# Two attention layers and two feed-forward layers on one core: tokens in two halves, attention units between the feed-forward steps

## The chip, the core and the metric

The kernel runs on one core of a Trainium2 chip. Its engines work side by side, each through its own list of instructions in order, and meet at semaphores: TensorE (PE, matrix products into the eight PSUM banks), VectorE (DVE), ScalarE (ACT), GpSimd (POOL, no PSUM) and SyncE (SP, here only DMA issues). The metric is the device time of one execution in microseconds.

## What is computed

Four residual steps on 1,024 tokens (16 sequences of 64) of width 256:

```python
x = x + tanh(g_xattn[0]) * L0_xattn(layernorm(x), ctx, ctx)
x = x + tanh(g_ffn[0])   * L0_ffn(layernorm(x))
x = x + tanh(g_xattn[1]) * L1_xattn(layernorm(x), ctx, ctx)
x = x + tanh(g_ffn[1])   * L1_ffn(layernorm(x))
...
# L0_xattn: 32 query heads of width 8 share 8 key heads; keys and values are ctx (64 keys)
# L0_ffn, hidden width 704, W = (wq - 128) * scale:
out = qlinear(silu(gate) * up, wq_down, s_down)
# L1_xattn: 16 query heads of width 16 share 4 key heads, then
out @ Wc.T + bc
# L1_ffn, 32 experts of inner width 96, every expert on every token:
sel_w, sel_e = top_k(x @ gate_w.T, 8); sel_w = softmax(sel_w)
h = silu(g) * u * masked_w[:, :, None]
out = einsum('tei,ehi->th', h, w_down_proj)
```

## The kernel before

It is written engine by engine, and the order on each engine is the order of the code. Four stages follow one another: attention of layer 0, its feed-forward, attention of layer 1, its experts.

*Attention.* Tokens lie in eight tiles of 128 (two sequences each). A tile has four units of work in layer 0 and two in layer 1. A unit is a chain: scores on PE (`scores`, L1055, two of 512 columns), row maximum and shift on DVE (L734, L739), exponential on ACT (L576), four transposes on PE (L1064), their copy on ACT (L582), four value products on PE (`values`, L1080). Per sequence DVE divides by the row sums (`normalise`, L754 and L762). Scores and transposes each use two banks in turn, and scores run two units ahead of the transposes. Per tile come the next layer's statistics (`next_stats`, `next_mean`, L780 to L784), a power on POOL for 1/std (L405), the normalised tile `xm` (L789), its transposes (L1105), and its split into a high and a low part, `xh` and `xl` (L435, L438 on POOL). POOL also makes the block-diagonal keys (`keys`, L337) and splits the queries (L412, L415). The statistics of the first normalisation (`ln_stats`, L709 to L714) are taken for six tiles at once ahead of the loop. `over_tiles` sets how the units of neighbouring tiles interleave; layer 1 adds a projection (L1096) and the routing logits (L1027).

*Feed-forward.* Full precision is made from three products (`product`, L1002 to L1004): high x high, high x low, low x high. The hidden width goes in chunks of 128 (6 in layer 0, 24 in layer 1), the tokens in two blocks of 512. One chunk on one block is a step: 6 products each for gate, up and down, down one step behind. ACT takes silu of the gate (L632) and rounds h to its high part `hh` (L655); DVE multiplies with up (L959, or L883 and then L888 with the expert mask) and makes the low part `hl` (L893). Weights stream in once, chunk by chunk; ACT rounds the high part `wh` (L551) and POOL subtracts the low part `wl` (L427), and both blocks use them. The accumulators of both blocks hold four banks; transposes bring the result back, and DVE adds it to x (L976).

*Routing.* Between attention and experts DVE picks the eight largest logits (L908 to L923); PE spreads the weights to 16 masks (L1177), which ACT and DVE copy to SBUF (L646, L935). They stay there, in `mbc`.

Of the kernel before, what the change touches and what calls it, by code (L numbers as in the profile page):

```python
# [23 lines left out]
NBLK = TOK // BLK  # L34
# [5 lines left out]
MOE_CHUNKS = EXPERTS * INNER // P  # L40
WPACK = 3 * DM
WRING = 3
# [3 lines left out]
FFN_CHUNKS = (HIDDEN + P - 1) // P  # L46
NEG = -3.0e38
W_EARLY = (TT - 2, TT - 1)
MASK_BANKS = (4, 7, 5, 6)
MASKS = NBLK * EXPERTS // EPQ  # L50
KEYS_AFTER = {3: (0, 2), 4: (2, 4), 5: (4, TT)}
AHEAD = 2


def after(eng, sem, value):

    if not (isinstance(value, int) and value <= 0):
# [61 lines left out]
class Attention:  # L119

    def __init__(self, layer, kv_heads, kbd, vbd, sb, sem):  # L130
# [1172 lines left out]
```

## Time and profile before

| | |
|---|---|
| runs | 450.45, 447.51, 449.8 us (median 449.8) |
| span of the profiled execution | 450.2 us; its own time is not listed apart, and the span lies within the runs |
| busy | PE 399.1, DVE 296.7, ACT 198.7, POOL 180.4 us |
| mean granted PE clock | 0.965 |

Records of PE overlap, since a product starts before the one ahead of it has drained, so its busy time is more than its work. On the other engines busy time is the sum of their instructions.

### The profile page before, as it was taken

How to read it: one execution, taken by the hardware profiler on the slowest of the kernel's cores; microseconds unless marked ns; L12 is line 12 of the kernel's file. 1: busy time of each engine (PE TensorE's matmuls, PEld its weight loads, DVE VectorE, ACT ScalarE, POOL GpSimd, SP SyncE). 2: the span in 40 equal slices, each digit the busy share in tenths (PEclk: the TensorE clock that was granted, in tenths of full speed). 3: DMA queues.
4: the chain of work that ended last, by engine and by line, in shares of the span. 5: the costliest groups of instructions: out<-in, count | busy, mean ns of one | idle time of the engine just before them, and what ended most of it. 6: DMA issues, size and time to landing. Idle time of an engine off the chain costs nothing.

```text
span 450.2 us, 6432 instructions
## 1 busy us (share of the span) xinstructions
PE 399.1 (89%) x2032; PEld 327.9 (73%) x2032; DVE 296.7 (66%) x554; ACT 198.7 (44%) x382; POOL 180.4 (40%) x174
## 2 busy tenths in 40 slices
PE   0598888959999778898877999999999999999994
PEld 0497777848888478787664887887887887887883
DVE  5989899843555778996465366566566566566554
ACT  6465455735444635554136333433433433333332
POOL 8776667561788353447500231131131121221200
PEclk9999899998999989999688899999999999999999
DMA  6500000110202000001100112112112011111002
GB/s 169 133 1 2 1 0 1 35 37 1 71 0 95 0 0 2 1 1 35 37 0 0 36 35 71 35 35 73 35 36 69 35 40 65 35 43 62 0 1 93
DMA packets 10711, 15.99 MB, mean 36 GB/s; under 512 B 4097, under 2 KB 6657, under 8 KB 10689
## 3 DMA queue, kind: packets, MB, share of 16 engines
q1 hardware_dynamic: 10688, 15.71, 11.8%
q8 instruction: 12, 0.20, 0.2%
q14 instruction: 11, 0.08, 0.1%
HBM read 14.66 MB, written 1.05 MB: 35 GB/s over the span
## 4 chain that ended last, share of the span: by engine, by line
PE 72%; DVE 15%; issue 5%; POOL 4%; ACT 2%; DVEq 1%; DMA 1%; POOLq 0%; ACTq 0%
PE bank L1002 19%; PE bank L1003 18%; PE bank L1004 18%; PE bank L1080 5%; PE bank L1055 4%; PE bank L1064 3%; DVE mx L734 2%; DVE dt_pt L739 2%; DVE xn L722 1%; POOL rstd L405 1%; DVE yt L762 1%; PE bank L1027 1%; DVE x L976 1%; PE bank L1040 1%; PE bank L1096 1%
## 5 line engine op out<-in xcount | busy, mean ns | idle before, releaser
L427 POOL TENSOR_TENSOR wl<-wraw,wh 128x768 fp32r<-128x768 f32 x24 | 44.7, 1863 | 162.2 <-ACT wh L551 162.2
L1002 PE MATMUL bank<-xh,wh 128*128 128x512 f32 x240 | 96.3, 401 | 0.0
L1003 PE MATMUL bank<-xl,wh 128*128 128x512 f32 x240 | 95.6, 398 | 0.0
L1004 PE MATMUL bank<-xh,wl 128*128 128x512 f32 x240 | 95.5, 398 | 0.0
L655 ACT ACTIVATE hh<-h_t 128x512 fp32r<-128x512 f32 x60 | 37.9, 632 | 114.9 <-DVE h_t L888 101.3
L893 DVE TENSOR_TENSOR hl<-h_t,hh 128x512 fp32r<-128x512 f32 x60 | 48.6, 810 | 42.7 <-ACT hh L655 42.7
L883 DVE TENSOR_TENSOR t_t<-bank,pts 128x512 f32<-128x512 f32 x48 | 33.2, 692 | 43.5 <-PE bank L1004 42.1
L888 DVE TENSOR_TENSOR h_t<-t_t,vbd 128x512 f32<-128x512 f32 x48 | 53.4, 1113 | 3.1 <-DVE t_t L883 1.0
L1055 PE MATMUL bank<-kbd,qt 128*128 128x256 f32 (+2 forms) x128 | 36.8, 395 | 20.2 <-DVE dt_pt L739 17.3
L1002 PEld LDWEIGHTS bank<-xh,wh 128*128 128x128 f32 x240 | 46.5, 194 | 9.9 <-issue 0.2
L1004 PEld LDWEIGHTS bank<-xh,wl 128*128 128x128 f32 x240 | 46.3, 193 | 10.1
L1003 PEld LDWEIGHTS bank<-xl,wh 128*128 128x128 f32 x240 | 46.3, 193 | 9.5
L1002 PE MATMUL bank<-hh,wh 128*128 128x512 f32 x120 | 50.4, 420 | 2.6 <-DVE hl L893 1.6
L1080 PE MATMUL bank<-vbd,pts 128*128 128x128 f32 (+1 forms) x384 | 52.3, 281 | 0.0
L1080 PEld LDWEIGHTS bank<-vbd,pts 128*128 128x128 f32 x384 | 49.3, 197 | 2.0 <-issue 0.3
L1003 PE MATMUL bank<-hl,wh 128*128 128x512 f32 x120 | 47.8, 398 | 0.0
L1004 PE MATMUL bank<-hh,wl 128*128 128x512 f32 x120 | 47.5, 396 | 0.0
L582 ACT ACTIVATE pts<-bank 128x256 f32<-128x256 f32 x96 | 31.6, 381 | 35.3 <-PE bank L1064 35.3
L1055 PEld LDWEIGHTS bank<-kbd,qt 128*128 128x128 f32 x128 | 19.9, 204 | 25.2 <-DVE dt_pt L739 7.6
L632 ACT ACTIVATE pts<-bank 128x512 f32<-128x512 f32 x48 | 28.3, 592 | 20.4 <-PE bank L1004 20.4
L734 DVE TENSOR_REDUCE mx<-bank 128x8 f32<-128x512 f32 x48 | 32.9, 685 | 2.0 <-PE bank L1055 1.2
L739 DVE TENSOR_TENSOR dt_pt<-bank,mx 128x512 f32<-128x512 f32 x48 | 33.1, 689 | 1.5
(104 smaller groups left out, 577.9 us busy)
## 6 DMA issues: line engine op xcount, KB each, us to landing
wraw<-w SPq DMA_DIRECT2D x30, 384.0 KB, 3.1
out<-x SPq DMA_DIRECT2D x8, 128.0 KB, 1.8
x<-x_in SPq DMA_DIRECT2D x1, 768.0 KB, 6.8
ctx_k<-ctx_t SPq DMA_DIRECT2D x2, 256.0 KB, 3.8
ctx_v<-ctx_in SPq DMA_DIRECT2D x2, 256.0 KB, 8.3
x<-x_in SPq DMA_DIRECT2D x1, 256.0 KB, 2.7
wc<-wc_t SPq DMA_DIRECT2D x1, 256.0 KB, 2.9
vbd<-sel_in SPq DMA_DIRECT2D x1, 256.0 KB, 3.5
```

What stands on the lines that cost most here:

```text
L427: nc.gpsimd.tensor_tensor(wl[:, cc % WRING, :], src[:, cc % 2, :], wh[:, cc % WRING, :].bitcast(F32), ALU.subtract).then_inc(m.w_split, 1)
L655: nc.scalar.activation(hh[:, k, :], h_t[:, k, :], ACT.Copy).then_inc(m.hh_ready, 1)
L734: chain.mark(nc.vector.reduce_max(mx[:, k, :], s, AX.X))
L739: nc.vector.tensor_tensor(dt_[:, k, :].rearrange("p (h t) -> p h t", t=KEYS), s, mx[:, k, :].unsqueeze(2).to_broadcast([P, 8, KEYS]), ALU. ...
L883: nc.vector.tensor_tensor(t_t[:], bank[2 + k][:], s_t[:, k, :], ALU.mult).then_inc(m.t_done, 1)
L888: nc.vector.tensor_tensor(h_t[:, k, :], t_t[:], mbc[:, q, k * BLK:(k + 1) * BLK], ALU.mult).then_inc(m.h_full, 1)
L893: nc.vector.tensor_tensor(hl[:, k, :], h_t[:, k, :], hh[:, k, :].bitcast(F32), ALU.subtract).then_inc(m.h_split, 1)
L1002: nc.tensor.matmul(o, wh[:, s, w_sl], rh, start=first, stop=False, skip_group_check=reopened)
L1003: nc.tensor.matmul(o, wh[:, s, w_sl], rl, start=False, stop=False, skip_group_check=reopened)
L1004: return nc.tensor.matmul(o, wl[:, s, w_sl], rh, start=False, stop=last, skip_group_check=reopened)
L1055: last = nc.tensor.matmul(bank[u % 2][:, i * a.ns:(i + 1) * a.ns], qt[:, b2, 2 * gp:2 * gp + 2, :].rearrange("p g s -> p (g s)"), a.kbd[:, ...
L1080: last = nc.tensor.matmul(bank[4 + b2][:, gp * P:(gp + 1) * P], pts[:, k, j, :], a.vbd[:, 2 * t + b2, pair, :], start=(pair == 0), stop=(p ...
```

## The change

The tokens go in two halves of 512. A feed-forward layer takes all its chunks for the first half and then again for the second: four passes, 60 steps (`PASS`: 0 to 5 and 6 to 11 for layer 0, 12 to 35 and 36 to 59 for layer 1). Attention is cut in ticks, one per unit and a few more to drain. Tables of numbers say which ticks stand after a step's gate products and which after its down products. Layer 0's ticks 0 to 21 run alone, 22 to 37 within steps 0 to 5; layer 1's ticks of the first half run within steps 9 to 11, the last six behind step 11 (`TAIL`), those of the second half within steps 16 to 32. DVE, ACT and POOL run one tick ahead of PE.

Layer 0's quantised weights are kept in six slots; layer 1's are loaded twice, and rounded and split twice. One bank each holds gate (`GB`), up (`UB`) and the mask, and two hold a pass's sum (`DB`), so that attention keeps banks of its own (`SB`, `PB`, `VB`, `MB`); up to unit 19 it borrows more to alternate. Silu is written with tanh, which takes one more instruction on DVE (`gate`). The mask of an expert group is spread into its bank when needed, and DVE reads it there (`weigh`). The low part of x moves to DVE (`x_low`); the first statistics are taken tile by tile; value blocks shrink from 128 to 72 columns; keys go in a ring of three tiles; all loops are written out.

```diff
-WRING = 3
-MASK_BANKS = (4, 7, 5, 6)
-AHEAD = 2
+HT = TT // 2
+VW = 72
+RING = 3
+SLOTS = 6
+WRAW = 3
+PASS = ((0, F0), (F0, 2 * F0), (2 * F0, 2 * F0 + MC), (2 * F0 + MC, 2 * F0 + 2 * MC))
+GB, UB, MASK = 0, 1, 7
+DB = ((2, 3), (2, 3), (2, 3), (4, 5))
+SB, PB, VB, MB = 4, 5, 6, 7
+TWO = 20
+ALONE = 22
...
+TAIL = ((11, 12), (13, 14, 15, 16))
+ROUTE = (13, 34)
...
+            def w_low(i):
+                src = wf[:, i % 2, :] if i < F0 else wraw[:, i % WRAW, :]
+                pool.wait_ge(F.wh_ready, i + 1)
+                slot = (i if i < F0 else i - F0) % SLOTS
+                ops.tensor_tensor(wl[:, slot, :], src, wh[:, slot, :].bitcast(F32), ALU.subtract
+                                  ).then_inc(F.w_split, 1)
...
-                    nc.scalar.activation(s_t[:, k, :], bank[k][:], ACT.Silu, scale=scale).then_inc(m.s_ready, 1)
+                nc.scalar.activation(s_t[:, s % 2, :], bank[GB][:], ACT.Tanh,
+                                     scale=sgh[:, c:c + 1] if s < MOE0 else 0.5).then_inc(F.s_ready, 1)
...
+            def x_low(a, t):
+                dve.wait_ge(a.xh_ready, t + 1)
+                tok = slice(t * P, (t + 1) * P)
+                ops.tensor_tensor(xl[:, :, tok], bank[a.x_bank(t)][:, 0:DM].rearrange("p (k c) -> p k c", c=P),
+                                  xh[:, :, tok].bitcast(F32), ALU.subtract).then_inc(a.xl_ready, 1)
...
+            def gate(s):
+                k = s % 2
+                dve.wait_ge(F.s_ready, s + 1)
+                ops.scalar_tensor_tensor(t_t[:, k, :], s_t[:, k, :], 1.0, bank[GB][:], ALU.add, ALU.mult
+                                         ).then_inc(F.sg_done, 1)
...
-                    nc.vector.tensor_tensor(h_t[:, k, :], t_t[:], mbc[:, q, k * BLK:(k + 1) * BLK], ALU.mult
-                                            ).then_inc(m.h_full, 1)
+                ops.tensor_tensor(h_t[:, k, :], bank[MASK][:], t_t[:, k, :], ALU.mult).then_inc(F.h_full, 1)
...
+            def tick0(n):
+                a, (t, u) = A[0], divmod(n, 4)
+                if u == 2 and t + 1 < TT:
+                    q_transposes(a, t + 1)
+                if u == 1 and 0 <= t - 2 < TT:
+                    x_transposes(a, t - 2)
+                if n + 1 < a.total:
+                    scores(a, n + 1)
+                if 0 <= n - 2 < a.total:
+                    values(a, n - 2)
+                if n < a.total:
+                    p_transposes(a, n)
...
+            q_transposes(A[0], 0)
+            scores(A[0], 0)
+            for n in range(ALONE):
+                tick0(n)
+            for s in range(STEPS):
+                gate(s)
+                if s in START:
+                    scores(A[1], START[s] * 2 * HT)
+                for k, n in beside(s, 0):
+                    tick(k, n)
+                up(s)
...
+                if s and s != MOE0:
+                    down(s - 1)
...
+                for k, n in beside(s, 1):
+                    tick(k, n)
...
+            down(STEPS - 1)
+            back(3)
```

PE at the passage from layer 0's attention to its feed-forward. In the rows 1055 and 1019 are scores, 1064 and 1037 transposes of a unit, 1080 and 1054 values, 1105 and 1090 transposes of x. Before:

```order
L1105 MATMUL bank<-ident,xm 128x128 x2
L1080 MATMUL bank<-vbd,pts 128x128 x4
L1064 MATMUL bank<-ident,dt_pt 128x128 x4
L1080 MATMUL bank<-vbd,pts 128x128 x8
L1105 MATMUL bank<-ident,xm 128x128 x2
L1002 MATMUL bank<-xh,wh 128x512
L1003 MATMUL bank<-xl,wh 128x512
```

And now, within step 1:

```order
L1153 MATMUL bank<-xh,wl 128x512
L1090 MATMUL bank<-ident,xm 128x128 x2
L1019 MATMUL bank<-kbd,qt 128x512 x2
L1054 MATMUL bank<-vbd,pts 128x72 x4
L1037 MATMUL bank<-ident,pt 128x128 x4
L1151 MATMUL bank<-xh,wh 128x512
L1152 MATMUL bank<-xl,wh 128x512
L1153 MATMUL bank<-xh,wl 128x512
L1151 MATMUL bank<-xh,wh 128x512
L1152 MATMUL bank<-xl,wh 128x512
L1153 MATMUL bank<-xh,wl 128x512
L1151 MATMUL bank<-hh,wh 128x512
```

Before, the products (1002 to 1004) began when the last units had drained; now transposes, scores and values of a unit (1090, 1019, 1054, 1037) stand between gate and up.

DVE in the expert stage; 883 and 862 multiply with up, 888 and 868 with the mask, 893 and 873 are the low part of h. Before:

```order
L893 TENSOR_TENSOR hl<-h_t,hh 128x512
L883 TENSOR_TENSOR t_t<-bank,pts 128x512
L888 TENSOR_TENSOR h_t<-t_t,vbd 128x512
L893 TENSOR_TENSOR hl<-h_t,hh 128x512
L883 TENSOR_TENSOR t_t<-bank,pts 128x512
```

And now, in step 17, with a unit of layer 1:

```order
L873 TENSOR_TENSOR hl<-h_t,hh 128x512
L850 SCALAR_TENSOR_TENSOR t_t<-s_t,bank 128x512
L862 TENSOR_TENSOR t_t<-bank,t_t 128x512
L868 TENSOR_TENSOR h_t<-bank,t_t 128x512
L730 TENSOR_REDUCE mx<-bank 128x8
L746 RECIPROCAL rc<-bank 128x8
L751 TENSOR_TENSOR yt<-bank,rc 64x2x4x16 x2
L736 TENSOR_TENSOR dt_<-bank,mx 128x512
```

A step has gained line 850, and behind the weighting stand the maximum, the division and the shift of a unit.

DVE at the end of layer 0's feed-forward; 985 and 880 scale the output, 976 and 887 add it to x, 709 to 714 and 711 to 716 are statistics. Before:

```order
L893 TENSOR_TENSOR hl<-h_t,hh 128x512
L976 TENSOR_TENSOR x<-bank,x 128x256 x2
L709 BN_STATS stats<-x 128x6 x2
L712 BN_AGGR mv<-stats 128x2 x2
L714 TENSOR_SCALAR ve<-mv 128x2
L985 TENSOR_SCALAR dt_pt<-bank,sdt 128x512
L722 TENSOR_SCALAR xn<-x,mv,rstd 128x4x4x16
L976 TENSOR_TENSOR x<-bank,x 128x256 x6
L722 TENSOR_SCALAR xn<-x,mv,rstd 128x4x4x16
L709 BN_STATS stats<-x 128x6 x6
L712 BN_AGGR mv<-stats 128x2 x6
L714 TENSOR_SCALAR ve<-mv 128x6
```

And now, behind step 11:

```order
L873 TENSOR_TENSOR hl<-h_t,hh 128x512
L880 TENSOR_SCALAR ot<-bank,sdt 128x512
L775 TENSOR_SCALAR xm<-x,mv,rstd 128x256
L781 TENSOR_TENSOR xl<-bank,xh 128x2x128
L761 SCALAR_TENSOR_TENSOR x<-bank,tg,xb 128x256
L767 BN_STATS stats<-x 128x6
L768 BN_AGGR mv<-stats 128x2
L769 TENSOR_SCALAR ve<-mv 128x1
L887 TENSOR_TENSOR x<-bank,x 128x256 x4
L711 BN_STATS stats<-x 128x6 x2
L714 BN_AGGR mv<-stats 128x2 x2
L716 TENSOR_SCALAR ve<-mv 128x2
```

Before, the second attention began here; now its first half ends here, and its last residual and statistics (761, 767) stand ahead of the additions and of the second half's statistics.

## Rows read from the trace of the kernel before

**Rows 1.** The page's totals: busy us, share of the span, instructions.
```profile
PE 399.1 (89%) x2032; PEld 327.9 (73%) x2032; DVE 296.7 (66%) x554; ACT 198.7 (44%) x382; POOL 180.4 (40%) x174
```

**Rows 2.** PE in order of time: start, us, engine, line, operation, tiles, shapes.
```profile
299.23 0.39 PE L1002 MATMUL bank<-xh,wh 128*128 128x512 f32 x1
...
300.59 0.39 PE L1002 MATMUL bank<-hh,wh 128*128 128x512 f32 x1
```

**Rows 3.** The chain of waits in layer 0's attention: start, us, engine, tile, line.
```profile
78.69 0.46 PE bank L1055 x2
...
79.59 0.89 PE bank L1080 x8
80.48 0.45 PE bank L1064 x4
```

**Rows 4.** The same chain at the routing logits.
```profile
201.62 2.14 PE bank L1027 x18
```

**Rows 5.** Busy time by stage: window, length, then each engine; PE's clock share, DMA.
```profile
18.50:101.50 83.00, 71.04 (x493) 62.67 (x493) 68.84 (x150) 46.63 (x114) 53.39 (x56) 0.98 0.04 11
101.50:151.10 49.60, 48.20 (x206) 39.50 (x206) 25.04 (x28) 24.73 (x37) 31.80 (x27) 0.97 0.12 38
151.10:220.00 68.90, 57.26 (x409) 51.42 (x409) 56.67 (x152) 33.70 (x80) 33.74 (x47) 0.96 0.04 12
220.00:247.30 27.30, 22.53 (x75) 15.65 (x75) 14.23 (x48) 11.69 (x22) 3.73 (x5) 0.75 0.00 0
247.30:439.00 191.70, 191.70 (x818) 153.32 (x819) 113.65 (x136) 69.40 (x113) 41.04 (x22) 0.99 0.13 41
```

**Rows 6.** Line 893 alone (DVE's low part of h) in one window.
```profile
252.00:435.00 183.00, 29.78 (x43) 1.00 0.14 43
```

**Rows 7.** Groups by line and shape: count, busy us, mean ns, idle before.
```profile
L427 POOL TENSOR_TENSOR wl<-wraw,wh 128x768 fp32r<-128x768 f32 x24 | 44.7, 1863 | 162.2 <-ACT wh L551 162.2
...
L959 DVE SCALAR_TENSOR_TENSOR h_t<-bank,su,pts 128x512 f32<-128x512 f32 x12 | 9.0, 750 | 14.9 <-PE bank L1004 14.9
```

**Rows 8.** DVE in order of time, layer 0's attention.
```profile
39.83 0.40 DVE L789 TENSOR_SCALAR xm<-x,mv,rstd 128x256 f32<-128x256 f32 x1
...
43.08 0.69 DVE L739 TENSOR_TENSOR dt_pt<-bank,mx 128x512 f32<-128x512 f32 x1
...
48.55 1.98 DVE L789 TENSOR_SCALAR xm<-x,mv,rstd 128x256 f32 x1 [0.55 <-POOL rstd L405]
...
53.37 0.69 DVE L739 TENSOR_TENSOR dt_pt<-bank,mx 128x512 f32<-128x512 f32 x1
...
66.08 0.26 DVE L754 RECIPROCAL rc<-bank 128x16 f32<-128x16 f32 x1
66.26 0.37 DVE L780 BATCH_NORM_STATS2 stats<-x 128x6 f32 x1
66.66 0.59 DVE L762 TENSOR_TENSOR yt<-bank,rc 64x128 f32<-64x128 f32 x2
67.28 0.69 DVE L739 TENSOR_TENSOR dt_pt<-bank,mx 128x512 f32<-128x512 f32 x1
67.89 0.17 DVE L783 BATCH_NORM_AGGREGATE mv<-stats 128x2 f32<-128x6 f32 x1
68.10 0.15 DVE L784 TENSOR_SCALAR ve<-mv 128x1 f32<-128x1 f32 x1
```

**Rows 9.** POOL in order of time, beside the second xm of rows 8.
```profile
48.48 1.90 POOL L337 TENSOR_TENSOR kbd<-kh,a_kmask 128x1024 f32 x1
```

**Rows 10.** ACT in order of time, the first exponential.
```profile
18.40 0.63 ACT L576 ACTIVATE dt_pt<-dt_pt 128x512 f32<-128x512 f32 x1 [0.56 <-DVE dt_pt L739]
```

**Rows 11.** SP's queue at the end.
```profile
444.66 3.79 SPq L393 DMA_DIRECT2D out<-x  x8
```

**Rows 12.** Busy time and clock around the first expert products.
```profile
217.40:227.60 10.20, 10.20 (x34) 8.32 (x34) 2.84 (x7) 0.77 (x2) 5.30 (x8) 0.50 0.00 1
```

**Rows 13.** Line 893 over the whole span: shortest, median and longest in ns.
```profile
L893 DVE TENSOR_TENSOR hl<-h_t,hh x60: 680/693/1914, 106.4 to 441.1; 128x512 fp32r<-128x512 f32 x60
```

More of the change, by code:

```diff
@@ L33 @@
 BLK = 512
-NBLK = TOK // BLK
 EXPERTS = 32
@@ new lines, in _ @@
+            act.wait_ge(k_loaded, 32)
+            copy(kh[:, 0:4], ctx_k[:, 0:4]).then_inc(kh_ready, 1)
+            copy(kh[:, 4:BATCH], ctx_k[:, 4:BATCH]).then_inc(kh_ready, 1)
+            q_copy(A[0], 0)
+            act.wait_ge(g_loaded, 32)
+            nc.scalar.activation(tg[:], tg[:], ACT.Tanh).then_inc(tanh_ready, 1)
+            act.wait_ge(tanh_ready, 1)
+            act.wait_ge(v_loaded, 32)
+            values(A[0])
+            for n in range(ALONE + 1):
+                tick0(n)
@@ new lines, in scores @@
+            def scores(a, n):
+                t = a.tile(n)
+                if n % a.units == 0:
+                    if a.layer == 0:
+                        pe.wait_ge(a.k_ready if t else k0_ready, 2 * t if t else 2)
+                    else:
+                        pe.wait_ge(a.k_ready, 2 * (t + 1))
+                    pe.wait_ge(a.q_ready, t + 1)
+                if a.before(n) >= 0:
+                    pe.wait_ge(a.sub_done, a.before(n) + 1)
+                if a.layer == 1 and n == 2 * HT:
+                    pe.wait_ge(a.xl_ready, HT)
+                b2, gps = a.part(n)
+                slot = (a.layer * TT + t) % RING
+                for i, gp in enumerate(gps):
+                    for r in range(2):
+                        done = nc.tensor.matmul(bank[a.s_bank(n)][:, i * a.ns:(i + 1) * a.ns],
+                                                qt[:, t % 2, b2, 2 * gp:2 * gp + 2, :].rearrange("p g s -> p (g s)"),
+                                                kbd[:, slot, r, b2, 0:a.ns], start=(r == 0), stop=(r == 1))
+                done.then_inc(a.scored, 1)
@@ new lines, in values @@
+            def values(a, n):
+                b2, gps = a.part(n)
+                t = a.tile(n)
+                q = 2 * t + b2
+                if n == 0:
+                    pe.wait_ge(a.v_ready, a.hk)
+                    pe.wait_ge(a.ones_ready, a.hk)
+                if gps[0] == 0 and a.v_before(q) >= 0:
+                    pe.wait_ge(a.y_done, a.v_before(q) + 1)
+                for j in range(4):
+                    gp, pair = gps[j // a.npair], j % a.npair
+                    if j in (0, 2):
+                        pe.wait_ge(a.pts_ready, 2 * n + 1 + j // 2)
+                    done = nc.tensor.matmul(bank[a.v_bank(q)][:, gp * P:gp * P + VW], pts[:, n % 2, j, :],
+                                            a.vbd[:, q, pair, :], start=(pair == 0), stop=(pair == a.npair - 1))
+                done.then_inc(a.av_done, 1)
```

1660 lines of the change are left out of this document (829 added, 831 removed).

## The prediction

> **What bounds the kernel now.** I first read the page's totals. PE counts as busy for 399.1 of 450.2 us [rows 1], but two records overlap, so I went by spacing: in the steady expert stage six products stand 1.36 us apart, 0.227 us each [rows 2]. A step (one hidden chunk, one block of 512 tokens) is 18 of them, 4.09 us. Twelve steps of layer 0 and 48 of layer 1 are 1,080 products, 245 us. A unit of attention takes 0.46 for scores, 0.89 for values and 0.45 for transposes [rows 3]; with the transposes of queries and of x, at 0.11 us per 128 columns by the last of these rows, it takes about 1.97, so 32 units are 63 us. Layer 1 has 16 units of about 1.9, plus per tile a projection of about 0.9 (an estimate: four records, each of twice the columns of a values record), logits of 6 x 0.119 [rows 4] and 0.9 of transposes: 50 us. Masks and the transposes back add 8. Together PE has 366 us of work, and 84 us in which it waits or runs slowly.
>
> The Trainium skill (Trainium Kernel Development and Optimization, Performance Expectations) calls matmul busy time a bad metric, because matmuls are pipelined. The trace agrees: by the busy row at most 51 us could be won, by spacing 84.
>
> The stages show where those 84 us lie [rows 5]. Layer 0's attention (18.5 to 101.5) holds 66 us of PE work (3 of them early products) in 83; there DVE is busy 68.84 and is the bound. Layer 0's feed-forward is 49.6 for about 45. From 151.1 to 220 the second attention holds some 50 in 68.9, with DVE busy for 56.67. Routing and masks (220 to 247.3) hold 13 in 27.3, at a mean clock of 0.75. The expert stage wastes little: 43 steps in 183 us, 4.26 each against 4.09 [rows 6]. The rest is the start (18.5) and the tail (11.2).
>
> **The change, part by part.** The work on PE stays the same. Values are written 72 columns wide instead of 128, which I count at nothing: logits with only 32 moving columns still take 0.119 us a record [rows 4], no less than the 0.111 of a values record (0.89 for 8). Reading the weights twice adds no visible wait while a step lasts 4 us: POOL's low part, 1.86 us [rows 7], is then due once per step instead of once per two, and the products of the step ahead hide it. Without that cover the 24 more of them would cost 24 x 1.86 = 45 us.
>
> *DVE* gets one instruction more per step, (tanh+1) x gate, at 0.75 like the nearest form [rows 7]: 60 x 0.75 = 45 us. In layer 0 it is all added. In layer 1, three full-width instructions and the low part are 0.75 + 3 x 0.7 = 2.85, less than a step. The mask now comes from PSUM and no longer from SBUF. Tanh and exp need no table switch: the new ScalarE order holds a single table load.
>
> *Attention alone (units 0 to 21).* One tile of before, from shift to shift, lasts 53.37 - 43.08 = 10.3 us [rows 8]. Inside it xm took 1.98 instead of the 0.4 it takes elsewhere, right behind POOL's key product [rows 8, 9]. After, each tile has its own statistics on DVE, three small instructions spaced 0.40 + 0.21 + 0.10 [rows 8] (before did six tiles at the start), and x's low part, a 128x256 read of PSUM, half a shift, so 0.4. A tile gets 10.3 + 0.75 + 0.4 + 0.2 for a scores product that is now one unit ahead instead of two = 11.6. At the start the first exponential (18.40, [rows 10]) moves little, since the work ahead of it stays; the shorter lead costs the first tile about 2, and I put tile 1 at 26.3. Tile 1 has no x of two tiles ago: 10.2. Tiles 2 and 4: 11.6 each. Tile 3: 11.6, plus 1.9 for the scale and selector preparation that moves here, plus 1.0 for a low-part product queued on POOL ahead of the addition that DVE waits for. Units 20 and 21 and the part of 22 that the first gate product waits for: 8.6. The first gate starts at 26.3 + 56.5 = 82.8.
>
> *Steps 0 to 5 with units 22 to 37.* In one step PE runs gate, unit n, up, down, units n+1 and n+2. Scores now have one bank, so scores of n+3 wait for the shift of n+2: that is maximum 0.6, normalise 0.8 to 0.9 and shift 0.6 on DVE behind the scores of n+2 [rows 8], and it ends some 1.3 us after PE has run out of other work. PE work of 4.09 + 3 x 1.97 = 10.0 becomes 11.1. Three such steps, then 7.4 for step 3 (units that only drain), 2 x 4.2, and 1.2 for the last low part of x: 50.3, to 133.1.
>
> *Steps 6 to 8.* 4.1; 4.1 + 2.1 for the transposes back of the first half, which alternate with DVE additions; 4.6. Sum 14.9, to 148.0.
>
> *Steps 9 to 11 with layer 1's first half.* Eleven units; the full ones cost DVE 1.25 for maximum and shift, 0.85 normalise, and up to 1.2 of residual, statistics and apply. One after another on single banks they take 8.4, 15.4 and 15.5 us where PE has 33: 39.3, to 187.3.
>
> *Drain and routing.* Six more units, the transposes back and the second half's statistics form one chain on DVE: low part, output scaling, last residual and its statistics, four additions, four statistics, apply, low part, logits. I count 13.8 us. Steps 12 and 13 cannot go down before the routing weights: 12.1 for 8.2 of products. To 213.2. Before paid from 149 to 163 and from 220 to 247 for the same things.
>
> *Steps 14 to 35 with the second half.* One unit per step. PE has 4.09 plus 1.0 to 2.8. DVE's loop for a heavy unit is 3.45 for the unit, then exp and tanh on ScalarE (0.63 each [rows 10], 1.45 with hand-over), then 0.75 + 0.7 + 0.7: 7.05. Only one unit is that heavy; the others are light on DVE or drain only, so PE sets them. By unit: 48.5 for eight steps, 47 for nine, 9.2 for the two ahead, 1.6 for masks, 14.4 for the last three with routing in them: 120.7, to 333.9.
>
> *Steps 36 to 59.* 24 x 4.09 + 8 masks x 0.23 + 1.6 for one way back = 101.7, to 435.6. Each gate waits for DVE's previous one, which ends some 1.1 us before it is needed, so the single banks cost nothing here.
>
> *The tail.* SP spends 3.79 us on eight stores [rows 11], now four are left at the end: 11.2 - 1.9 = 9.3 behind the last up product, which ends 1.2 before the step does: 443.7.
>
> *Clock.* Before ran at half clock (1.2 GHz) throughout 217.4 to 227.6 [rows 12], after 4 us of sparse transposes. The drain at 187 to 213 is just as sparse. I add 3 us, with bounds of 0 (no lower clock where PE is critical) and 7 (10 us like these, at half rate, less what DVE hides). Sum 446.7 against its own span of 450.2, to which next to nothing lies around it; the median of the runs shown is 449.8, 0.4 below it. I forecast **446 us**.
>
> So the profit is only 4 us: the way from attention to feed-forward and routing gets shorter, and layer 0's attention pays some of it back, because the woven units still go at DVE's pace.
>
> **Rivals.** (a) *Weaving hides fully.* If DVE keeps ahead of PE in every woven step, steps 0 to 5 take 45.6, 9 to 11 33 and 14 to 35 116: 15 us less, 431. For it: DVE is busy for only about two thirds of the span. Against: DVE is nearly gapless in today's attention, and the scores bank is single.
>
> (b) *Weaving hides nothing.* Slower: in steps 0 to 2, 10, 11 and 18 to 23 the unit's DVE round simply adds to the 4.09 us, as it stands alone today: 10 units at 2.6 (10.3 / 4) and 16 at 3.3 instead of what I charged, 16 us more, 462. It decides where scores of unit n+1 wait for the shift of n before PE has a product left to run. Against it: gate, up and down stand between most units.
>
> (c) *POOL's low part blocks DVE's.* hl took 0.69 as a rule and 1.91 at worst [rows 13]. With a POOL product in every step, a late one would hold hl until it ends; h_split then comes 0.3 us too late beyond its slack of 0.9. At 48 steps that is 14 us, 461. By my order POOL's ends 0.2 us before hl is due, so it must run over 1.1 us late first. The Trainium skill (SBUF — State Buffer, SBUF: two separate sides) states this as an exclusive lock for a whole instruction between GpSimd and a DVE instruction with two SBUF inputs; by that rule the mask in PSUM frees the weighting, but hl stays exposed, now twice as often. The trace agrees that the two meet: xm took 1.98 behind a POOL product of 1.90 [rows 8, 9].
>
> (d) *It doesn't do what it says*, for instance a tick order that puts waits on banks that make halves serial. I see none in the order; 0.03.
>
> **How the numbers follow.** Forecast as summed, with its own range of 440 to 453 from the clock's bounds and 4 us either way for hand-worked steps: 0.45. (a) 0.22, (b) 0.22, (c) 0.08, (d) 0.03. About 1%, or 4.5 us, can be told from no change. Of the forecast's range four tenths lie below 445.3, so faster is 0.18 + 0.22 = 0.40; the other six tenths are same, 0.27; (b), (c), (d) are slower, 0.33. The range of 8 in 10 reaches to (a) and close to (b): 430 to 464.
>
> **What the profile after would show.** Right: the first product of a gate near 83 us, step 14 near 213, step 36 near 334, steps of 4.1 us from there, DVE gapless in the units alone, PE waiting for the shift in steps 0 to 2. Wrong: tiles alone under 10.5 or over 12.5; woven steps at PE's sum (a) or at PE plus DVE (b); hl well over 0.8 us in the last 24 steps (c); half clock longer than 10 us between 187 and 213.

## The result and the profile after

The changed kernel takes 475.57 us (median of 4 runs, 474.91 to 478.26) against 448.65 (median of 4, 447.51 to 450.45): the ratio is 1.059, with a 95% interval of 1.055 to 1.064. The forecast was 446, with a range of 430 to 464. The profiled execution has a span of 473.7 us and took 475.5.

The page's totals, which answer to [rows 1]:

```profile
PE 406.9 (86%) x2032; PEld 332.1 (70%) x2032; DVE 324.6 (69%) x638; ACT 205.5 (43%) x388; POOL 203.7 (43%) x181
```

All engines are busier in sum, and none has become a bound for the whole. Busy time by stage, as in [rows 5], cut where the first gate product of steps 0, 6, 9, 14 and 36 starts, at 187.20, where PE has done the products within step 11 and goes on with ticks 8 to 10, and at 464.50, behind the products of step 59. Columns: window, length, PE, PEld, DVE, ACT, POOL, granted clock, DMA share, GB/s.

```profile
0.00:82.26 82.26, 54.25 (x326) 47.23 (x327) 63.48 (x137) 47.51 (x104) 65.53 (x72) 0.92 0.29 79
82.26:136.50 54.24, 48.52 (x272) 41.27 (x272) 35.34 (x76) 22.77 (x48) 10.57 (x14) 0.94 0.01 1
136.50:151.39 14.89, 13.99 (x67) 11.35 (x67) 10.52 (x22) 4.49 (x7) 2.34 (x3) 1.00 0.00 0
151.39:187.20 35.81, 30.27 (x190) 26.49 (x188) 25.43 (x55) 18.79 (x40) 19.05 (x21) 0.95 0.05 13
187.20:230.96 43.76, 28.04 (x115) 21.41 (x113) 23.02 (x70) 7.71 (x16) 9.36 (x10) 0.71 0.09 27
230.96:359.83 128.87, 124.24 (x608) 99.97 (x607) 94.68 (x174) 57.42 (x103) 57.16 (x42) 0.98 0.22 68
359.83:464.50 104.67, 104.37 (x449) 82.54 (x447) 68.82 (x102) 45.51 (x70) 39.71 (x22) 1.00 0.26 77
464.50:473.70 9.20, 3.26 (x15) 1.87 (x14) 3.31 (x7) 1.32 (x2) 0.00 (x0) 0.90 0.17 58
```

Set against the forecast's own sums:

| stretch | forecast | measured |
|---|---|---|
| to the first gate product | 82.8 | 82.3 |
| steps 0 to 5 | 50.3 | 54.2 |
| steps 6 to 8 | 14.9 | 14.9 |
| steps 9 to 13, drain and routing of the first half | 65.2 | 79.6 |
| steps 14 to 35 | 120.7 | 128.9 |
| steps 36 to 59 | 101.7 | 104.7 |
| tail | 8.1 | 9.2 |
| clock, apart | 3 | in the rows above |
| span | 446.7 | 473.7 |

Half of the miss lies in steps 9 to 13. The forecast has three terms for them: steps 9 to 11 with ticks 0 to 10 (8.4 + 15.4 + 15.5 = 39.3), the drain (13.8), steps 12 and 13 (12.1). Cut at the start of step 11, at the end of tick 10 (the projection at 194.25 in the chain below) and at the first product of step 12, with the columns as above:

```profile
151.39:175.11 23.72, 19.95 (x138) 17.60 (x135) 17.04 (x37) 13.15 (x27) 13.95 (x16) 1.00 0.06 18
175.11:196.16 21.05, 16.95 (x89) 14.04 (x87) 12.05 (x31) 6.39 (x15) 6.35 (x7) 0.82 0.07 19
196.16:215.71 19.55, 10.29 (x44) 8.05 (x45) 9.36 (x29) 2.18 (x5) 3.25 (x3) 0.67 0.08 21
215.71:230.96 15.25, 11.13 (x37) 8.22 (x37) 9.99 (x29) 4.79 (x8) 4.85 (x5) 0.72 0.10 26
```

Steps 9 and 10 took 23.7 us, as forecast (8.4 + 15.4). Step 11 took 21.1 instead of 15.5, the drain 19.6 instead of 13.8, steps 12 and 13 15.3 instead of 12.1, and in these three the granted clock was 0.82, 0.67 and 0.72. What PE waited for from 187.2 to 230.96 (us in total, times, longest):

```profile
PE bank L1108 <- DVE xl L781: 7.4, 4, 3.5
PE bank L1151 <- DVE hl L873: 4.7, 2, 2.6
PE bank L1239 <- DVE wts L917: 1.5, 1, 1.5
PE bank L1220 <- DVE x L887: 1.4, 1, 1.4
```

The logits (1108) wait for the low part of x, tile by tile, and the products for the low part of h. The chain of waits there, start, us, what:

```profile
192.79 1.46 PE bank L1108 x6
194.25 1.91 PE bank L1077 x4
196.25 0.49 DVE x L761
196.77 0.44 DVE stats L767
197.52 0.69 DVE hl L873
...
203.32 0.84 PE bank L1108 x6
...
208.23 0.76 DVE stats L711 x2
209.54 0.66 DVE stats L711 x2
210.69 0.41 DVE xm L775
...
214.41 1.46 PE bank L1108 x6
```

The work passes from PE to DVE and back in pieces of half a microsecond to two. The six logits of a tile take 1.46 at 192.79 and 214.41 and 0.84 at 203.32: half clock (1.2 GHz) and full. Before, the same chains of projection, logits and routing are [rows 4] and [rows 12]; there eight tiles passed through them in a row. How long the drain is, PE's last transposes of a unit show, before and in the first half of the kernel after:

```profile
210.69 0.60 PE L1064 MATMUL bank<-ident,dt_pt 128*128 128x128 f32 x4
...
227.83 0.26 PE L1027 MATMUL bank<-gwh,xl 128*128 128x32 f32 x1
```

```profile
182.25 1.12 PE L1037 MATMUL bank<-ident,pt 128*128 128x128 f32 x4 [1.14 <-ACT pt L553]
```

From there to the end of the last logits (228.1 before, 215.9 after) it is 17.4 us before, with 12 products of the expert stage in it, and 33.6 us after, with 18 products of steps 10 and 11 in it.

What shows against the single steps of the forecast: the added instruction, line 850, takes 687 ns (first row), and the low part of h is as long as in [rows 13] in most steps, but has a longer worst case (second row; shortest, median and longest in ns).

```profile
L850 DVE SCALAR_TENSOR_TENSOR t_t<-s_t,bank x60: 673/687/691, 87.1 to 462.6; 128x512 f32<-128x512 f32 x60
L873 DVE TENSOR_TENSOR hl<-h_t,hh x60: 674/693/2352, 93.4 to 465.6; 128x512 fp32r<-128x512 f32 x60
```

And PE around a mask (1239) in step 36, in order of time:

```profile
362.33 0.39 PE L1153 MATMUL bank<-xh,wl 128*128 128x512 f32 x1
362.65 0.50 PE L1239 MATMUL bank<-wts,sel 64*128 64x512 f32 x1
363.07 0.51 PE L1151 MATMUL bank<-hh,wh 128*128 128x512 f32 x1
363.42 0.40 PE L1152 MATMUL bank<-hl,wh 128*128 128x512 f32 x1
363.65 0.40 PE L1153 MATMUL bank<-hh,wl 128*128 128x512 f32 x1
```

The starts are 0.23 apart between equal products, but 0.32, 0.42 and 0.35 around the mask: it costs 0.32 + 0.42 + 0.35 - 2 x 0.23 = 0.63, not one product of 0.23.

### The profile page after: what moved, and what is told of

It reads as the page before. It is cut to its first block, busy times and chain, and to the rows that moved or that the text cites. A ratio compares the mean times of both kernels' runs of the same rounds, so it can differ in the third digit from the quotient of the medians.

```text
span 473.7 us, 6122 instructions
## 1 busy us (share of the span) xinstructions
PE 406.9 (86%) x2032; PEld 332.1 (70%) x2032; DVE 324.6 (69%) x638; ACT 205.5 (43%) x388; POOL 203.7 (43%) x181
## 4 chain that ended last, share of the span: by engine, by line
PE 72%; DVE 16%; POOL 5%; issue 3%; ACT 2%; DMA 1%; DVEq 0%; POOLq 0%
PE bank L1151 18%; PE bank L1152 17%; PE bank L1153 17%; PE bank L1054 6%; PE bank L1019 4%; PE bank L1037 3%; DVE dt_ L736 3%; POOL kbd L338 2%; PE bank L1077 2%; DVE xm L775 2%; PE bank L1108 2%; PE bank L999 2%; PE bank L1239 1%; DVE hl L873 1%; DVE yt L751 1%
## 5 line engine op out<-in xcount | busy, mean ns | idle before, releaser
L436 POOL TENSOR_TENSOR wl<-wraw,wh 128x768 fp32r<-128x768 f32 x48 | 89.2, 1860 | 85.0 <-ACT wh L532 85.0
L1151 PE MATMUL bank<-xh,wh 128*128 128x512 f32 x240 | 100.2, 417 | 3.7 <-POOL wl L436 1.8
L850 DVE SCALAR_TENSOR_TENSOR t_t<-s_t,bank 128x512 f32<-128x512 f32 x60 | 41.1, 686 | 33.0 <-ACT s_t L632 32.4
L1054 PEld LDWEIGHTS bank<-vbd,pts 128*128 128x128 f32 x384 | 52.6, 203 | 4.9 <-DVE yt L751 1.8
L730 DVE TENSOR_REDUCE mx<-bank 128x8 f32<-128x512 f32 x48 | 33.1, 689 | 33.1 <-PE bank L1019 32.6
L1054 PE MATMUL bank<-vbd,pts 128*128 128x72 f32 x384 | 51.9, 281 | 1.3 <-DVE yt L751 1.3
L632 ACT ACTIVATE s_t<-bank 128x512 f32<-128x512 f32 x48 | 28.6, 596 | 45.8 <-PE bank L1153 45.8
L1019 PE MATMUL bank<-kbd,qt 128*128 128x512 f32 (+1 forms) x128 | 36.5, 390 | 12.9 <-DVE dt_ L736 11.1
L1037 PE MATMUL bank<-ident,pt 128*128 128x128 f32 x192 | 33.6, 303 | 16.2 <-ACT pt L553 14.7
L409 POOL TENSOR_TENSOR rstd<-ve,neghalf 128x1 f32<-128x1 f32 x16 | 10.9, 680 | 76.8 <-DVE ve L769 76.8
L553 ACT ACTIVATE pt<-dt_ 128x512 f32<-128x512 f32 x48 | 30.3, 632 | 27.7 <-DVE dt_ L736 27.4
## 6 DMA issues: line engine op xcount, KB each, us to landing
out<-x SPq DMA_DIRECT2D x8, 128.0 KB, 2.6
```

Of the source, the lines that this page charges most:

```text
L436: ops.tensor_tensor(wl[:, slot, :], src, wh[:, slot, :].bitcast(F32), ALU.subtract).then_inc(F.w_split, 1)
L553: nc.scalar.activation(pt[:, n % 2, :], dt_[:, n % 2, :], ACT.Exp, scale=a.scale).then_inc(a.p_ready, 1)
L730: return chains[a.layer].mark(ops.reduce_max(mx[:, n % 2, :], s, AX.X))
L850: ops.scalar_tensor_tensor(t_t[:, k, :], s_t[:, k, :], 1.0, bank[GB][:], ALU.add, ALU.mult).then_inc(F.sg_done, 1)
L1019: done = nc.tensor.matmul(bank[a.s_bank(n)][:, i * a.ns:(i + 1) * a.ns], qt[:, t % 2, b2, 2 * gp:2 * gp + 2, :].rearrange("p g s -> p (g s)"),
L1037: done = nc.tensor.transpose(bank[a.p_bank(n)][:, j * P:(j + 1) * P], pt[:, n % 2, j * P:(j + 1) * P], ident[:])
```

## The experiments

Theory A: layer 1's first half loses the time. Its chain from the last units to the first masks has too little beside it, and PE has more to do elsewhere than I had counted. Theory B: DVE's added work made the kernel slow. Theory C: weaving costs as much as it hides. The medians of the kernel before, taken with each group of runs, lie between 448.65 and 452.02 us, so the ratios to it are compared, and the lengths of stages in the traces. These vary too where an edit touches nothing: the first gate product falls between 81.5 and 85.5 us, steps 0 to 5 take 51.0 to 55.8, steps 9 to 13 78.2 to 81.0, steps 14 to 35 128.7 to 129.5. A difference inside such a range tells nothing; the forecast's 50.3 for steps 0 to 5 lies just outside of its range.

**The added instruction.** It is cut to one column, and the product with up takes tanh alone.

```diff
-ops.scalar_tensor_tensor(t_t[:, k, :], s_t[:, k, :], 1.0, bank[GB][:], ALU.add, ALU.mult
+ops.scalar_tensor_tensor(t_t[:, k, 0:1], s_t[:, k, 0:1], 1.0, bank[GB][:, 0:1], ALU.add, ALU.mult
```

> The kernel after with the extra DVE instruction of a step cut from 512 columns to one; the product with up then takes tanh alone, so (tanh+1) x gate is left out of the computation. It takes 59 x 0.6 = 35 us off DVE and hurts nothing else. Theory A (PE starves in the chain from the first half's last units to its masks, 187 to 231, and elsewhere has more work than I counted; DVE's load is not the bound): 466 to 472, since the instruction lies on a path only in the woven steps 0 to 5 and 9 to 11 and at two steps of the drain. Theory B (DVE's load, raised by this instruction, is what made the kernel slow): 455 or less.

475.06 us, ratio 1.052 (1.047 to 1.057). Steps 0 to 5 took 52.3 instead of 54.2, steps 9 to 13 79.5, steps 14 to 35 128.0. Theory B is out: 35 us taken from DVE give back 1.9, 0.1 and 0.9 us, and only the last is more than such stretches vary by. The 466 to 472 that stood with theory A was missed as well: even in the woven steps the instruction costs less than expected.

**Layer 0's units alone.**

```diff
-TWO = 20
-X_TWO = 4
-ALONE = 22
-BESIDE0 = {0: ((22,), (23, 24)), ...
+TWO = 32
+X_TWO = 8
+ALONE = 38
+BESIDE0 = {}
```

> The kernel after with all 38 ticks of layer 0 alone and two banks each to the end of layer 0's units, none beside steps 0 to 5. Woven, these six steps took 54.2 us after the first gate product at 82.3. Theory A: ten more units at 2.6 us (10.3 / 4), 3 us of drain and 6 x 4.1: step 6 begins near 136, the kernel takes 473 to 478, so weaving in layer 0 hides about nothing. Rival (weaving hides what DVE leaves open): step 6 begins at 145 or later, 484 or more. Third (the single banks of the woven units cost more than they hide): step 6 before 131, 470 or less.

476.22 us, ratio 1.055 (1.051 to 1.058). The first products of steps 0 and 6, in order of time (the file's lines are one less):

```profile
110.20 0.78 PE L1150 MATMUL bank<-xh,wh 128*128 128x512 f32 x1
...
135.71 0.39 PE L1150 MATMUL bank<-xh,wh 128*128 128x512 f32 x1
```

Step 6 starts at 135.7 instead of 136.5 (134.7 to 141.1 in woven runs with no edit in layer 0). In layer 0 the weave gains nothing that can be told. The run gives the units two banks each as well, so it doesn't separate what the weave hides from what its single banks cost.

**The second half's units alone.**

```diff
-BESIDE2 = {s: ((), (s - 16,)) for s in range(16, 33)}
+BESIDE2 = {16: ((), tuple(range(17)))}
```

> The kernel after with the 17 ticks of layer 1's second half all behind step 16, none beside steps 17 to 32. Woven, steps 14 to 35 took 128.9 us, of which 22 x 4.09 = 90 are products, and PE had hardly a wait. Theory A (here the weave hides DVE's rounds under the products): alone a tick goes at DVE's pace and 17 of them take 50 to 56 us instead of the some 29 that they add woven: 495 to 502. Rival (the weave hides nothing here either): 473 to 480.

497.41 us, ratio 1.099 (1.095 to 1.103). The first products of steps 16 and 17:

```profile
244.71 0.39 PE L1151 MATMUL bank<-xh,wh 128*128 128x512 f32 x1
...
301.07 0.77 PE L1151 MATMUL bank<-xh,wh 128*128 128x512 f32 x1
```

The 17 ticks take 56.4 - 4.1 = 52.3 us alone. Steps 14 to 35 took 151.2 instead of 128.9: here the weave does what it is for, and saves 22 us. Theory C holds for layer 0 only. The run tells more: eight units of one half, alone, take 52.3 us, while before 16 units took 68.9 [rows 5]. The two don't compare at the same clock: from 273.5 to 301.1, behind the last unit's transposes, PE ran at half clock in run e4, and was busy for 18.1 of these 27.6 us. At full clock it would be up to 9 us less (an estimate, half of the 18.1), 43 for half the units; so up to 9 of the 22 us are what the weave saves by keeping the clock up.

**The order in the drain.** First the second half's statistics go behind the routing (`route(0)`), then behind step 12's low part, then the ticks are spread, then both.

```diff
                     add_back(1)
-                    ln_stats(A[1], HT, HT + 2)
-                    ln_stats(A[1], HT + 2, TT)
                     for n in TAIL[1]:
...
-BESIDE1 = {9: ((), (0, 1)), 10: ((2, 3), (4, 5)), 11: ((6, 7), (8, 9, 10))}
-TAIL = ((11, 12), (13, 14, 15, 16))
+BESIDE1 = {9: ((0,), (1, 2, 3)), 10: ((4, 5, 6), (7, 8)), 11: ((9, 10), (11, 12))}
+TAIL = ((13, 14), (15, 16))
```

> The kernel after with the second half's statistics on DVE moved behind the first half's routing; they stood ahead of the normalisation of the first half's last tile (208.2 to 210.7). Theory A (the chain to the first masks is the bound there): 2.4 us less, 473. Rival (DVE waits for something else there, or the second half needs its statistics early): no change or slower, 475 to 478.

> The kernel after with the second half's statistics on DVE moved behind the low part of step 12 in step 13, where no step waits for them; behind the routing (run e3) they stood still ahead of step 12's instructions on DVE. Theory A: steps 11 to 14 take 53.4 us instead of 55.85, the kernel 473. Rival (that DVE time is not on the path, e3 moved nothing because something else ends there): 55.5 or more, 475 to 477.

> The kernel after with the ticks of layer 1's first half placed earlier among steps 9 to 11, so that products of steps 10 and 11 stand between the light ticks 11 to 14 that ran without cover. In after PE waited 5.5 us from step 9 to 187.2 and 15.7 from there to step 14. Theory A (the drain has no products to cover it): step 12 begins 5 to 10 us sooner after step 9 than the 64.3 us of after, the kernel takes 466 to 471. Rival (the rounds over DVE, ACT and POOL set the pace of every tick, wherever the products stand): what the drain saves the ticks ahead of it lose, step 9 to 12 stays at 62 to 66 us, 474 to 478.

> Runs e5 and e7 together. Theory A: both gains add, 463 to 469. Rival: 473 to 477.

None of the first three reached what theory A forecast. Behind the routing: 475.27 us, ratio 1.052 (1.050 to 1.055); steps 11 to 13 took 56.2 instead of 55.9, since the statistics still stood ahead of step 12 on DVE. Behind step 12: 474.41, ratio 1.051 (1.043 to 1.059); steps 11 to 13 54.3 (53.4 forecast), steps 9 to 13 77.9, hardly outside what they vary by. Spread: 472.40, ratio 1.050 (1.043 to 1.058); steps 9 to 13 75.8; step 12 begins 59.7 us behind step 9, 4.6 sooner, where theory A had 5 to 10 and the rival at most 2. Both: 468.67, ratio 1.038 (1.031 to 1.046); steps 9 to 13 (cut at step 12):

```profile
151.31:210.33 59.02, 46.88 (x268) 39.08 (x265) 37.34 (x86) 21.71 (x47) 23.88 (x26) 0.87 0.07 21
210.33:225.90 15.57, 11.85 (x36) 8.94 (x37) 10.87 (x38) 4.79 (x8) 2.54 (x2) 0.72 0.09 26
```

Together 74.6 instead of 79.6. That meets the forecast (463 to 469). Order gives back 5 of the 14.4 us that were missed.

**The clock in the drain.** Products that nobody reads are put where PE waited; then the same with run e8's order.

```diff
+def filler(k, o):
+    if o == GB:
+        pe.wait_ge(F.sg_done, MOE0)
+    for _ in range(k):
+        nc.tensor.matmul(bank[o][:], wh[:, 5, 0:P], xh[:, 0, BLK:2 * BLK], start=True, stop=True, ...)
...
+filler((4, 5, 12, 5)[t], GB)      # in logits of tiles 0 to 3
+filler(7, GB)                     # ahead of the last down product
+filler(4, GB)                     # ahead of back(1)
+filler(12, DB[2][0]), filler(6, ...), filler(8, ...)   # in step 13, around the routing
```

> The kernel after with 63 products more on PE, written to a bank that nobody reads before it is begun anew, at those places from 191 to 228 where PE waited (4 to 12 in each). They keep PE busy where it ran at half clock (1.2 GHz) from 198 to 219 and from 228 to 233. If the half clock costs what its records say (logits 1.46 instead of 0.84 per tile, projection 1.9 instead of 1.0, products 0.43 instead of 0.23): step 12 to 14 and the drain get 6 to 10 us shorter, 466 to 470. Rival (the lower clock falls only where PE waits for DVE anyway, or the products get in the way): 474 to 480.

> Run e8 with the filling products of run e6 (the four ahead of the first logits left out, 59 products). If the clock and the order are separate costs of the drain, both gains add: 461 to 465. If the better order has taken the same waits that the filling products fill, 466 to 470.

With filling alone 468.12 us, ratio 1.036 (1.028 to 1.043), and with both 467.09, ratio 1.037 (1.029 to 1.045). Steps 9 to 11 and 12 to 13, the filling alone:

```profile
151.94:211.60 59.66, 50.80 (x305) 42.66 (x303) 38.42 (x96) 21.52 (x47) 23.54 (x26) 0.97 0.07 21
211.60:227.02 15.42, 14.53 (x64) 10.86 (x64) 10.22 (x29) 4.79 (x8) 3.64 (x4) 1.00 0.08 27
```

And with run e8's order:

```profile
150.58:210.06 59.48, 51.97 (x300) 43.44 (x299) 37.17 (x86) 21.71 (x47) 23.88 (x26) 0.94 0.07 21
210.06:225.11 15.05, 14.56 (x64) 10.86 (x63) 10.70 (x34) 4.79 (x8) 2.02 (x2) 1.00 0.09 26
```

The clock is 0.97 and 0.94 in steps 9 to 11 and full in 12 and 13, against 0.84 and 0.72 in the kernel after; yet the stretch is 75.1 and 74.5 us, as with the order alone (74.6). The gains don't add. With filling, steps 14 to 35 took 126.4 in both, against 128.9 and, in run e8, 129.6. That is the clock: run e7, without filling, took 126.4 as well, and in all three the granted clock of this stretch was 1.00, against 0.98 in the kernel after and 0.97 in run e8.

**The masks.**

```diff
-if s > MOE0 and (s - PASS[pass_of(s)][0]) % CPQ == 0:
+if s == PASS[3][0]:
     spread(s)
```

> The kernel after with one mask per half, that of the first expert group, instead of eight: 14 products with the selector are left out, and the other experts are weighted by the wrong mask. By the rows of steps 36 to 59 a mask costs 0.64 us (steps with one last 4.73 instead of 4.09): 9 us less, 466 to 468. By the 0.23 that I had charged: 3.2 us less, 472. A third way, if the reading of the mask in PSUM holds DVE up, more than 12 us less, 463 or under.

472.83 us, ratio 1.048 (1.040 to 1.056). From the first product of step 36 to that of step 59 it takes 460.38 - 364.36 = 96.0 instead of 100.6 us, for seven masks: 0.66 each, so the row was right and my 0.23 wrong. Steps 14 to 35 gained nothing in the profiled execution (128.8 us), which was the longest of the four (475.36): PE was busy there for 2.3 us less and waited as much longer. So the 9 us less did not come, and the whole time is nearer to the 472 that went with 0.23: the price of a mask is shown by steps 36 to 59, not by the median.

**Layer 0's tiles.** Three edits to find what makes a tile of the units alone 11.1 to 13.7 us long, against 10.3 [rows 8]: scores two ahead; POOL's low part of the weights cut to one column; DVE's low part of x cut to one.

```diff
-if n + 1 < a.total:
+if TWO <= n and n + 1 < a.total:
     scores(a, n + 1)
...
+if n + 2 <= TWO:
+    scores(a, n + 2)                # behind p_transposes
```

```diff
+n = 1 if i < F0 else 3 * DM
-ops.tensor_tensor(wl[:, slot, :], src, wh[:, slot, :].bitcast(F32), ALU.subtract
+ops.tensor_tensor(wl[:, slot, 0:n], src[:, 0:n], wh[:, slot, 0:n].bitcast(F32), ALU.subtract
```

```diff
+n = 1 if a.layer == 0 else P
+tok = slice(t * P, t * P + n)       # x_low, and the same n for the bank's columns
```

> The kernel after with the scores of layer 0's units up to 20 issued two units ahead, behind the transposes of the unit, as in the kernel before, instead of one ahead. Alone, a tile took 11.1 to 13.7 us against 10.3 before, and DVE waited 1.14 us for scores behind each transpose of queries. If the short lead is what the tile lost: 1 to 1.5 us per tile, first gate product at 76 to 78 instead of 82.3, 470 to 472. Rival (DVE's own work per tile, raised by statistics, low part and scales, sets the pace): first gate product at 81 or later, 474 to 477.

> The kernel after with POOL's low part of layer 0's weights cut to one column; PE takes the high part in its place in layer 0's third products, so that the computation lacks the weights' low part there. It takes six instructions of 1.83 to 1.86 us from POOL under ticks 4 to 19, where POOL was busy for two thirds of the time and DVE's xm took 1.3 to 1.7 instead of 0.41 us beside POOL. If this preparation, which the change moved under the units, is what made a tile longer than before: first gate product at 75 to 78 instead of 82.3. Rival (POOL's keys alone hold xm, the low part falls into gaps): 81 or later.

> The kernel after with DVE's low part of x in layer 0 cut to one column per 128; PE takes the high part in its place in layer 0's second products, so that the computation lacks x's low part there. It takes 0.4 us from DVE for each of the four tiles whose low part falls before the first gate product, and 0.4 for each of the others. If DVE's own work sets the pace of the units alone: first gate product 1 to 1.6 us sooner than 82.3. Rival (the waits between the engines set it): no change within 0.5, beyond what the start of a run moves.

The first gate product came at 81.8, 80.7 and 84.2 us, where it varies between 81.5 and 85.5 without an edit; the times were 476.86, 475.64 and 472.81 (ratios 1.061, 1.059, 1.049, each with 0.008 either way). In each the rival held by this sign, which varies by more than run e13 was to give. The tiles themselves tell more, from the shift of a tile's first unit to that of the next (736, in run e12 737). Tile 3, the longest, after and in run e12:

```profile
49.03 0.69 DVE L736 TENSOR_TENSOR dt_<-bank,mx 128x512 f32<-128x512 f32 x1
...
62.76 0.69 DVE L736 TENSOR_TENSOR dt_<-bank,mx 128x512 f32<-128x512 f32 x1
```

```profile
48.36 0.69 DVE L737 TENSOR_TENSOR dt_<-bank,mx 128x512 f32<-128x512 f32 x1
...
60.65 0.69 DVE L737 TENSOR_TENSOR dt_<-bank,mx 128x512 f32<-128x512 f32 x1
```

It takes 13.7 us, in the runs with e9's and e13's edit too, and 12.3 in run e12: POOL's low part of the weights costs 1.4 there, and the scales and the selector, prepared on DVE from 49.6 to 51.3, another 1.7. These are the two extras that the prediction charged to tile 3 (1.0 and 1.9). The lead and DVE's low part are worth nothing that can be told. The tiles before it are 11.2 and 11.1 us long, the one behind it 12.1 (11.0 in several runs); before, four tiles from 32.94 on took 10.1, 10.3, 11.5 and 10.2. Counted by shifts, the kernel after is 6.0 us late with 12 units done (49.03, before 43.08 [rows 8]) and 9.4 with 16 (62.76, before 53.37).

**Lighter products** in steps 0 to 5 and 9 to 11.

```diff
+if light[0]:
+    return nc.tensor.matmul(o, wh[:, slot, w_sl], rh, start=first, stop=stop, skip_group_check=True)
...
+light[0] = s < F0 or 9 <= s < MOE0
```

> The kernel after with one matrix product instead of three (high x high alone, the low parts are left out of the computation) in steps 0 to 5 and 9 to 11: 68 products less in the first stretch (15.5 us at 0.2275), 40 less in the second (9.1 us). If PE is the bound of the woven steps: steps 0 to 5 take 38 to 41 instead of 54.2 us, and from step 9 to 12 it takes 55 to 58 instead of 64.3. If the units' rounds over DVE and ACT set the pace: 0 to 5 still take 47 or more, 9 to 12 62 or more.

462.88 us, ratio 1.029 (1.022 to 1.036). The first products of steps 0, 6, 9 and 12:

```profile
84.07 0.47 PE L1154 MATMUL bank<-xh,wh 128*128 128x512 f32 x1 [0.93 <-issue]
...
129.32 0.80 PE L1155 MATMUL bank<-xh,wh 128*128 128x512 f32 x1 [1.71 <-DVE xl L781]
...
146.34 0.48 PE L1154 MATMUL bank<-xh,wh 128*128 128x512 f32 x1
...
205.77 0.77 PE L1155 MATMUL bank<-xh,wh 128*128 128x512 f32 x1
```

Steps 0 to 5 took 45.3 us, 9 less for 15.5 us of products; step 9 to 12 took 59.4, 4.9 less for 9.1. Neither theory's range was met: somewhat more than half of the products' time came back. The rest was hidden under the units' rounds or went to the clock: from step 9 to 14 the mean granted clock was 0.76, against 0.82 in the kernel after. The three full steps with units went from 10.9, 12.7 and 13.1 to 10.8, 10.2 and 10.2 us: a floor that three units' rounds over DVE and ACT, at 3.4 us each, would set (this is argued, no run shows it).

**Filling in the kernel before.** The clock also falls there [rows 12].

```diff
+filler(8, 0)       # ahead of the last transposes of y
+filler(10, 7)      # ahead of the transposes of the routing weights
```

> The kernel before with 18 products more on PE that nobody reads, 8 ahead of the last transposes of y at 214 to 216 and 10 ahead of the transposes of the routing weights at 231 to 233, where PE waited just before it ran at half clock (217.4 to 227.6, 234.5 to 237.9). If they keep the clock up: 12 products at 0.23 instead of 0.43, 12 logits at 0.11 instead of 0.21 and more, 4 to 6 us less, ratio 0.987 to 0.992. Rival (the products delay what stands behind them, or the clock falls all the same): ratio 0.997 to 1.005.

451.0 us against 451.17, ratio 1.002 (0.998 to 1.006). Granted clock in windows of 3 us:

```profile
217.00:220.00 3.00, 2.76 (x16) 1.96 (x14) 1.25 (x4) 0.38 (x1) 1.53 (x3) 1.00 0.01 3
220.00:223.00 3.00, 1.12 (x10) 0.90 (x9) 1.29 (x2) 0.38 (x1) 2.37 (x4) 1.00 0.00 0
223.00:226.00 3.00, 3.00 (x13) 2.52 (x13) 0.00 (x0) 0.00 (x0) 1.09 (x2) 0.61 0.00 0
226.00:229.00 3.00, 3.00 (x9) 2.42 (x10) 2.47 (x21) 0.72 (x2) 0.00 (x0) 0.50 0.00 0
```

The clock held at 217 to 220, PE then had little to do until 223 and fell to half speed behind that. The second place went the same way: from 234.5 to 237.9 the clock was now full, but it was half from 240.7 to 251.0, before from 244.7 to 251.5. The half clock moved, and nothing was won. None of the versions tried beats the kernel before.

## Why the prediction was wrong

**The first stages were right.** The first gate product was due at 82.8 and came at 82.3; steps 6 to 8 were met. That the first is so close is partly luck: its terms are off by up to 1.2 us each and cancel (tile 1 took 11.2 instead of 10.2, tile 3 13.7 instead of 14.5, the end 7.4 instead of 8.6), and the sign of a gapless DVE in the units alone did not come: from 26 to 82 it was busy for 47.84 of 56 us and waited 4.0 for scores. Layer 0 was forecast to lose, and did. At 151.4 the kernel after has done what the kernel before had done at 151.1 less three steps: 12.6 us behind. Most of that is lost in the units alone (9.4 us by their 16th), not in the weave. Runs e2 and e14 fit a weave that can't win there: PE itself needs 1.97 for a unit and a unit alone takes some 2.6, so 16 units leave little to hide; that the rounds on single banks eat it is argued, since no run changes the banks alone. This is rival (b), in layer 0.

**The step that failed** is the one on steps 9 to 11 with the paragraph "Drain and routing", 39.3 + 13.8 + 12.1 = 65.2 us. It measured 79.6: steps 9 and 10 as forecast, step 11 5.6 us longer, the drain 5.7 and steps 12 and 13 3.1. I had said that before "paid from 149 to 163 and from 220 to 247 for the same things", and so took the new drain for a shorter one. It is the longer one, 33.6 us against 17.4 for twice the units: nine of a half's 17 ticks hold no unit of their own. The change pays this twice. The second time it stands under 17 steps of products; the first time only five steps are at hand, and they are too few. I had counted DVE's instructions and hand-overs for the last tile; in the trace they stand behind one another for every tile: at 187.3 the rounded h of step 11 was there, but its low part ran at 197.5, behind the projections, residuals and statistics of two tiles. And PE's share of the chain ran in part at half clock (granted clock 0.67 in the drain).

The edits take single things away: full clock gives 4.5 us (e6), a better order 5.0 (e8), both together 5.0 (e11), 9.1 us of products less 4.9 (e14, 146.3 to 221.0), and DVE's extra instruction less 0.1 (e1). The first four end at 74.5 to 75.1 us, 9 above the forecast. That fits a chain of hand-overs that none of them shortens, but it is not shown: run e14 ran at a lower clock, and no edit shortened the chain itself. The low part of h of step 11, moved ahead of the two tiles on DVE, would be one to try.

**Steps 14 to 35**: the weave hid DVE there, as rival (a) had it (PE waited 4.6 us in 128.9, and run e4 is 22 slower in this stretch). But the 120.7 was built on 4.09 per step. Added up by the distances from one start to the next, the 395 products in the trace of this stretch took 97.4 us, 0.247 each instead of 0.2275: 7.6 us more, which is nearly all of the 8.2 missed. In it are the wider spacing where products follow another kind of work (0.32 for the first one), the masks' neighbours, and stretches at half clock, which runs e6 and e7 show to be worth 2.5. So the term was mis-sized, its mechanism right.

**Steps 36 to 59**: eight masks at 0.64 instead of 0.23, 3.3 us, as run e10 confirms. Mis-sized.

**The clock**: 3 us added with a bound of 7. From 187.2 to 231 the mean clock was 0.71, which is 25 us at half rate; taking it away gave 4.5 there and 2.5 later. That is the bound itself, and more than twice the 3 charged; and the sign of being wrong, half clock for longer than 10 us between 187 and 213, came (191.9 to 202.1, and again from 209.0 to 219.2).

**The hidden parts** were hidden: line 850, as far as run e1 can tell, the second reading of the weights (PE waited for POOL's low part once in steps 14 to 35, 1.8 us). Rival (c), POOL's low part against hl, showed in three woven steps with hl at about 2 us, and PE waited 1.5 us for hl in steps 14 to 35; from step 36 on, where it was forecast, not at all. What (c) says of the mask held: before, the weighting (888, both inputs in SBUF) took 1.52 to 1.73 us instead of 0.69 in 21 of 48 steps, each time beside POOL's low part; now, with the mask read from PSUM (868), all 48 take 0.68 to 0.69. So DVE spends 20 us less on it (33.1 instead of 53.4).

**Against the kernel before** the account is: layer 0 12.6 us worse (shown by the stage times; of tile 3 the cause is shown, 1.4 by run e12 and 1.7 by the rows of the scales, for the rest of the units alone it is open, since neither e9 nor e13 accounts for it); from 151 on 313.1 us instead of 287.9, of which three more steps are 12.3, so 12.9 worse; the tail 2.0 better. That is the 23.5 us between the spans. The range failed because the stretches of layer 1 all erred to the same side.

## What to carry to other kernels

A chain that passes through several engines has a fill and a drain that need not shrink when the work is halved (17.4 us before, 33.6 here); before a pass is split, read them from the trace and name the independent work that stands under each copy. Weaving can win at most what one engine waits for beyond its own work: some 0.6 us a unit in layer 0, but 22 us in the expert steps, where a half took 52 us alone, in part at half clock. And price an instruction put between others by the distances of the starts around such a place, not by its length in a run of equals.

## What was not expected of the hardware

The mask product with 64 rows costs 0.63 to 0.66 us among 128-row products that stand 0.23 apart. A full clock paid in some places and not in others: in steps 12 to 13 the granted clock went from 0.72 to 1.00, and these took 15.4 instead of 15.3 us; in steps 9 to 11 it went from 0.84 to 0.97 and they took 59.7 instead of 64.3; behind the better order it gave nothing (74.5 against 74.6 for both). Filling PE's waits in the kernel before only moved the half clock, from 217 to 223 and from 245 to 241 us.
